# Expert routing of a two-layer decoder issued at other steps of the loop before it

## The reference

```python
x = _layernorm(x + attention(x))                       # phase 0: 16 heads
x = _layernorm(x + cross_attention_L0(x, context))     # phase 1: 16 heads, a norm of its own inside
x = _layernorm(x + experts_L0(x))                      # phase 2: top 2 of 8, GELU, hidden 512
x = _layernorm(x + gated_decay_attention(x))           # phase 3
x = _layernorm(x + cross_attention_L1(x, context))     # phase 4: 8 heads
x = _layernorm(x + experts_L1(x))                      # phase 5: top 1 of 8, ReLU, hidden 256

# experts_L0, its routing
router_logits = jnp.einsum('bth,eh->bte', x, router_w)
topk_values, topk_indices = jax.lax.top_k(router_logits, 2)
topk_weights = jax.nn.softmax(topk_values)
```

## Time and profile before

| what | value |
|---|---|
| median of 3 runs | 1522.08 us (1520.77 to 1522.19) |
| the profiled execution | 1532.61 us, of which the span of its instructions is 1530.8 us |
| PE, busy share of the span | 83% |
| ACT, busy share | 55% |
| DVE, busy share | 52% |
| POOL, busy share | 35% |
| mean granted TensorE clock | 0.927 of full |

### The profile page before, as it was taken

How to read it: one execution, slowest core, us unless ns; L and a number is a source line. 1 busy time by engine, 2 the same in 40 slices (tenths; PEclk the granted TensorE clock), 3 DMA queues, 4 the chain that set the end, 5 groups by cost and what they waited for, 6 DMA issues and landing times. The chain is left out here.

```text
span 1530.8 us, 22554 instructions
## 1 busy us (share of the span) xinstructions
PE 1276.4 (83%) x6934; PEld 735.2 (48%) x6934; DVE 801.0 (52%) x2448; ACT 839.1 (55%) x1902; POOL 530.0 (35%) x606
## 2 busy tenths in 40 slices
PE   5999999999999988877861994899999996786452
PEld 2334443444344335545431993576676764454251
DVE  3543454354334435366653235878675766567425
ACT  4777677767767753554430563567575653453121
POOL 2554455545545531212243351132223222112332
PEclk9999999999999999999885997999999997997686
DMA  8335343330000000000013671100000000000053
GB/s 211 57 62 83 63 71 60 57 80 1 1 1 1 1 1 0 1 1 0 3 58 131 195 208 48 42 1 1 1 1 1 1 1 28 0 1 8 23 153 100
DMA packets 77556, 67.29 MB, mean 44 GB/s; under 512 B 5024, under 2 KB 68640, under 8 KB 77184
## 3 DMA queue, kind: packets, MB, share of 16 engines
q1 hardware_dynamic: 73488, 57.69, 16.6%
q0 software_dynamic: 3520, 7.27, 1.3%
q10 hardware_dynamic: 432, 0.89, 0.2%
HBM read 37.42 MB, written 28.41 MB: 43 GB/s over the span
## 5 line engine op out<-in xcount | busy, mean ns | idle before, releaser
L1960 POOL TENSOR_TENSOR work<-work 128x512 f32<-128x512 f32 x256 | 266.1, 1039 | 271.6 <-DVE work L1438 271.6
L1013 ACT ACTIVATE work<-bank,work 128x512 f32<-128x512 f32 x256 | 176.5, 689 | 116.7 <-DVE work L1430 116.7
L1430 DVE TENSOR_REDUCE work<-bank 128x1 f32<-128x512 f32 x256 | 176.6, 690 | 77.5 <-PE bank L547 77.5
L555 PEld LDWEIGHTS bank<-cst,work 128*128 128x128 f32 x1024 | 110.4, 141 | 163.8 <-issue 103.5
L555 PE MATMUL bank<-cst,work 128*128 128x128 f32 x1024 | 159.7, 283 | 6.3 <-ACT work L1021 6.1
L1438 DVE RECIPROCAL work<-work 128x1 f32<-128x1 f32 x256 | 41.9, 164 | 223.4 <-ACT work L1013 223.1
L1021 ACT ACTIVATE work<-bank 128x512 f32<-128x512 f32 x256 | 152.6, 596 | 0.5 <-PE bank L555 0.5
L547 PE MATMUL bank<-work 64*128 64x512 f32 x512 | 144.5, 641 | 3.4 <-ACT work L1013 3.4
L2000 POOL TENSOR_TENSOR work<-work 128x1232 f32<-128x1232 f32 (+1 forms) x32 | 55.5, 1734 | 254.9 <-DVE work L1512 254.8
L565 PE MATMUL bank<-work 128*64 128x512 f32 x512 | 137.4, 617 | 0.7 <-ACT work L1021 0.7
L494 PE MATMUL bank<-OT,W 128*128 128x512 f32 x208 | 95.7, 604 | 1.2 <-DVE am L1618 0.7
(11 more groups left out here) (258 smaller groups left out, 2443.6 us busy)
## 6 DMA issues: line engine op xcount, KB each, us to landing
xs<-gat SPq DMA_DIRECT2D x18, 1040.0 KB, 13.1
W<-in_w SPq DMA_DIRECT2D x30, 322.0 KB
W<-in_w SPq DMA_DIRECT2D x23, 193.0 KB
work<-xs SPq DMA_DIRECT2D x62, 65.0 KB
gat<-yt SPq DMA_DIRECT2D x12, 256.0 KB, 3.4
work<-in_w SPq DMA_DIRECT2D x9, 322.0 KB
W<-in_v SPq DMA_DIRECT2D x1, 2048.0 KB, 12.3
x_ext<-in_x SPq DMA_DIRECT2D x4, 256.0 KB, 7.5
```

Of the source, the lines that this page charges most:

```text
L555: m = nc.tensor.transpose(out[:, k * P:(k + 1) * P], pA[u % 5][:, k * P:(k + 1) * P], ident)
L1013: A(pA[u % 5], bank[u % 3][:, :], ACT.Exp, bias=nmax[:, u % 8:u % 8 + 1], accum_out=rsum[0][:, u % 8:u % 8 + 1]).then_inc(sem("a_e"), 1)
L1430: V.tensor_reduce(nmax[:, u % 8:u % 8 + 1], bank[u % 3][:, :], AX, ALU.max, negate=True)\
L1960: G.tensor_tensor(pA[u % 5], pA[u % 5], rsum[1][:, u % 8:u % 8 + 1].to_broadcast([P, S]), ALU.mult)\
```

## The change

`cross` and `moe` issue the same instructions in another order; no operation is added or dropped. A piece in table form (steps u of the cross loop; "moe" is the head of the expert phase):

| piece | before | after |
|---|---|---|
| logits of batches 0, 1 (PE) | end of 11, 15 | end of 10, 14 |
| route1 of 0, 1 (DVE) | 12, 16, behind the tail pieces | 11, 15, ahead of them |
| exp of 0, 1 (ACT) | end of 12, 16 | end of 11, 15 |
| route2 of 0, 1 (DVE) | 13, 17 | 12, 16 |
| prefix of 0, 1 (PE) | end of 14, 18 | end of 13; 16 in phase 1, 17 in phase 4 |
| rank of 0, 1 (DVE) | 15; moe | 14; 16 in phase 1, 17 in phase 4 |
| scatter of batch 0 (POOL) | whole at 15 | half at 15, half at 16 |
| turn_x of batch 2 (PE, ACT) | 18 | 17, ahead of the output pairs of batch 3 |
| logits of batch 2 (PE) | moe | 17, between the second and the third output pair |
| prefix of 2 (PE) | behind the last output product | phase 2: ahead of it; phase 5: unchanged |

```diff
+        PREFIX_AT = {2: (13, 16), 5: (13, 17)}
+        RANK_AT = {2: (14, 16), 5: (14, 17)}
@@ cross_tail
-                        tail(w0 + b, s)
+                        if (b, s) != (NB - 2, 8):
+                            tail(w0 + b, s)
@@ PE, cross_out
-                for p in range(np_):
+                for p in pairs:
@@ PE, cross
-                    if t == 1 and b >= 1:
-                        cross_out(c, b - 1)
-                    if u in (11, 15):
+                    if u == PREFIX_AT[ph + 1][1]:
+                        moe_prefix(MOE[ph + 1], 1)
+                    if u == NB * NT + 1:
+
+                        tail(w0 + NB - 2, 8)
+                        cross_out(c, NB - 1, range(0, 2))
+                        moe_logits(MOE[ph + 1], NB - 2)
+                        cross_out(c, NB - 1, range(2, c["np"]))
+                    elif t == 1 and b >= 1:
+                        cross_out(c, b - 1, range(c["np"]))
+                    if u in (10, 14):
                         moe_logits(MOE[ph + 1], u // 4 - 2)
-                    if u in (14, 18):
-                        moe_prefix(MOE[ph + 1], u // 4 - 3)
+                    if u == PREFIX_AT[ph + 1][0]:
+                        moe_prefix(MOE[ph + 1], 0)
@@ PE, moe
-                moe_logits(m_, 2)
+                if ph == 2:
+                    moe_prefix(m_, 2)
                 tail(m_["w0"] - 1, 0)
-                moe_prefix(m_, 2)
+                if ph == 5:
+                    moe_prefix(m_, 2)
@@ ACT, cross
+                    if u == NB * NT + 1:
+                        tail(w0 + NB - 2, 8)
                     if t == 1 and b >= 1:
                         cross_o(c, b - 1)
-                    if u in (12, 16):
-                        moe_exp(MOE[ph + 1], u // 4 - 3)
+                    if u in (11, 15):
+                        moe_exp(MOE[ph + 1], u // 4 - 2)
@@ DVE, cross
+                    if u in (11, 15):
+                        moe_route1(MOE[ph + 1], u // 4 - 2)
                     cross_tail(tail, w0, u)
                     if u in (12, 16):
-                        moe_route1(MOE[ph + 1], u // 4 - 3)
-                    if u in (13, 17):
                         moe_route2(MOE[ph + 1], u // 4 - 3)
-                    if u == 15:
-                        moe_rank(MOE[ph + 1], 0)
+                    if u in RANK_AT[ph + 1]:
+                        moe_rank(MOE[ph + 1], RANK_AT[ph + 1].index(u))
@@ DVE, moe
-                moe_rank(m_, 1)
@@ POOL, cross
-                    if u == 15:
-                        moe_scatter(MOE[ph + 1], 0)
+                    if u in (15, 16):
+                        moe_scatter(MOE[ph + 1], 0, (0, 1) if u == 15 else (2, 3))
```

More of the change, by code:

```diff
@@ L657, in cross_turn, with cross_out @@
                     m.then_inc(sem(n + "_t"), 1)
-            def cross_out(c, b):
+            def cross_out(c, b, pairs):
                 n, np_ = c["n"], c["np"]
@@ L2002, in cross, with moe_scatter @@
                     cross_tail(tail, c["w0"], u)
-                    if u == 15:
-                        moe_scatter(MOE[ph + 1], 0)
-            def moe_scatter(m_, b):
+                    if u in (15, 16):
+                        moe_scatter(MOE[ph + 1], 0, (0, 1) if u == 15 else (2, 3))
+            def moe_scatter(m_, b, tiles=range(NT)):
                 pool.wait_ge(sem("M_idx"), m_["b0"] + b + 1)
@@ L2010, in moe_scatter @@
                     loaded(pool, "zero", DMA_COUNT["zero"])
-                for t in range(NT):
+                for t in tiles:
                     for k in range(m_["k"]):
```

## The result

The changed kernel took 1538.9 us (median of 4 runs, 1536.2 to 1541.3) against 1522.1 for the kernel before: ratio 1.0109, 95% interval 1.0093 to 1.0124. That is 16.8 us slower, with 14.2 to 18.9 as its interval; 21.7 was predicted, with a range that held the result. Its profiled execution took 1541.26 us, 1539.4 of it span.

The account below looks back on a forecast made before the run. PE was taken to be bound by waits for ACT, DVE and POOL in turn, not its own work. Terms 4.0 + 10.3 + 4.4 + 3.0 = 21.7 on 1522.1 gave 1544 us; range 1527 to 1551.

Parts of the forecast that it names:

- steps 1 to 4: Phase 1, up to DVE's unit 15: PE waits for shared banks' readers and ACT's copies; unit 15 comes 7.7 us later.
- steps 5, 6: Phase 1, after unit 15: POOL wins 7 us, but turn_x holds the pairs; batch 3's output product starts 5.0 us later.
- Step 7: End of phase 1: rank 2 is done before the last product's sum, -1.0 us.
- A page against a row: Whether scatter transfers hold DVE's normalisation: nothing by the trace rows, up to 4 us by the documented rule read widely.
- the narrow reading: POOL holds DVE's two-SBUF-input instructions only during its multiply, so the halved scatter costs DVE nothing.
- The clock: Phase 1: granted clock falls in four waits, each slowing the PE work behind it by 2.6 us, +10.3 in all.
- phase 1's sum: Phase 1 in total: +4.0 us without the clock and +10.3 us for the clock.
- Phase 4: The same waits with half the heads: batch 3's output product 4.4 us later, plus 3.0 us for the clock.
- the likeliest case: Whole kernel: new waits and slow clock behind them give 1544 us, bounds 1536 to 1551, chance 0.65.
- the waits come but the clock holds: Rival for both phases: clock falls at most once or twice; 8.4 us slower, up to 15, 1530 to 1536; chance 0.18.
- The faster rival: Bank readers finish in time and POOL's freeing pays: 5.5 to 10.4 us faster, 1512 to 1517; chance 0.11.
- steps 1 and 3: Phase 1 bank waits: second query product behind the logits copy, +4.3 us; batch 2's output product behind the rank, +7.5 us.

Follow-up runs that it names:

- e9: Changed kernel with shorter groups of unused PE products issued ahead of its waits, fewer in phase 4: 1542.1 us, 1.0134.
- e2: Changed kernel with logits and prefixes in PSUM bank 5 instead of a turn of banks 6 and 7: 1525.2 us, 1.0018.
- e4: Changed kernel with batch 0's rank ahead of DVE's subtraction of unit 14 instead of behind it and the norm: 1531.9 us, 1.0056.
- e10: Changed kernel with batch 0's logits, route1, exp and route2 back at their old steps: 1534.1 us, 1.0077.
- e1: The kernel before, run and profiled again without edit: 1522.6 us, 0.9996.
- e7: Changed kernel with logits 0, 1 and prefixes in bank 5 and the end of the cross phase in its old order: 1512.6 us, 0.9930.
- e12: Changed kernel with batch 0's scatter issued whole at step 15: 1543.9 us, 1.0149.
- e5: Changed kernel with unused PE products meant to fill its long waits; in the turns they stood behind the wait: 1538.7 us, 1.0116.
- e6: The kernel before with unused PE products meant to fill its long waits; in the turns they stood behind the wait: 1540.1 us, 1.0122.
- e8: Changed kernel with bank 5 for logits 0, 1 and prefixes, the old cross-phase end, and the scatter whole at step 15: 1522.1 us, 0.9993.
- e11: Changed kernel with turn_x and logits of batch 2 behind the last output pairs on PE and ACT: 1540.8 us, 1.0116.
- e3: The kernel before with logits and prefixes in bank 5: 1524.6 us, 1.0006.

## Why the prediction was right, and where its sizes were off

**The order of takes (steps 1 to 4): right.** Counted from DVE's unit 11 (701.4 in the working, 698.24 in the trace), the output product of batch 2 should start 48.0 later and unit 15 60.5 later. They came at 50.8 and 65.9. The products behind the first two waits ran 1.2 (8.27 for e9's 7.02) and 1.4 (7.22 for e9's 5.84) longer than at full clock, and the output product 2.6 (9.66 for 7.03); less these it is 48.2 and 60.7. e2, e4 and e10 show the cause: each wait goes with its own edit and takes its time with it.

**POOL freed, the pairs held by turn_x (steps 5, 6): right, one term missing.** POOL won its 7 us (e2: 7.2). From unit 15 to the end of `x_ext` the sum had 24.0; it took 26.3 (764.17 to 790.44). The 1.9 us for multiply 15 holding L1352 was right (2.10 for 0.16), but the same hold on L1575 (1.86 for 0.17) and on L1637 (1.02 for 0.22) was missing: 2.5 us. By the sum's own times multiply 14 starts at +4.8, just when DVE comes to route1, and the earlier trace rows showed what a multiply does to an instruction with two SBUF inputs.

**Step 7: right.** -1.0 predicted, -1.2 in B against e1.

**A page against a row: the trace decides for the narrow reading.** DVE's short instructions under the four transfers of 779 to 784 take 0.16 to 0.22 us, so the second half of the scatter costs DVE nothing. The held ones all overlap a multiply of POOL. That is what the Trainium skill, GPSIMD Engine Reference, "Key points", says of instructions with two SBUF inputs, and the Trainium skill, SBUF — State Buffer, "SBUF: two separate sides", says more narrowly that whichever of the two engines starts first has the shared ports for its whole instruction; the trace agrees (2.10 us for 0.16, ending with the multiply). One row does not fit so simply: L1353 of the earlier trace rows starts at 773.12, beside the last transfer and 0.56 us ahead of the multiply's recorded start at 773.68, and is held all the same. Which of the two had begun first is not shown, since spans on POOL are rough.

**The clock: the place right, the size too large.** Four falls of 2.6 were summed as +10.3. In the profile they cost 1.2, 1.4, 2.6 and, behind `turn_x`, 2.4 (12.3 us from the end of `x_ext`, 790.44, to the product, for 9.9 in the sum): 7.6. The term took the dearest fall of the earlier trace rows for each. Against that the earlier trace rows already held a fall at 678.15 that the changed kernel's execution did not have (5.67 for 8.27). So A closes, with the terms as the trace has them: 118.15 + 5.0 + 7.6 + 2.5 - 2.6 = 130.65, for 130.66 measured. That phase 1's sum came out so near (14.3; 14.1 with the clock and the holds as measured) is in part luck: the clock was put 2.7 us too high, and the missing holds 2.5 too low.

**Phase 4: too large.** 4.4 + 3.0 was predicted. The waits came as worked out: 1.99 for the query product (2.1), 3.30 for the output product (3.6), the pairs behind prefix 1 and rank 1. Counted from the start of C the output product came 7.6 us later than before (6.0 in the sum, which left the clock out) and the pairs 8.4 (5.5). Two things were less than the sum had them. The clock's term counted 1.75 for a slow output product behind its wait, and that one ran in 3.67 at a granted clock of 1.00 (1405 to 1415). And the clock came back earlier at the end than in the earlier trace rows: from the start of the last pairs to the last output product it is 6.76 us (9.50 before, 8.4 in the sum), so C grew by 5.6, and this product ran in 3.70, where it took 5.35 in the earlier trace rows and 5.36 in e1, so D shrank by 1.8. The sum had no term for a fall that goes away. Net 3.8 for 7.4.

Together the four stretches give 14.7 us for 21.7, and the medians 16.8. The result lies in the likeliest case's own bounds (1536 to 1551), near the end that had half of the clock's part. The rival "the waits come but the clock holds" falls for phase 1, where a slow product follows each of the waits; in phase 4 it is half right. The faster rival falls for the changed kernel, as steps 1 and 3 cost 13.7 us where it needed under 8. With them gone its time of 1512 to 1517 still did not come (e2: 1525.2), since `turn_x` holds the pairs. It was reached only with the end in its old order as well (e7: 1512.6).

**Open.** The 2.7 us (0.6 to 5.0) by which e2 is slower than the kernel before, though its stretches A to D are 2.2 us shorter than e1's in sum; and why e12 loses 5 us by the medians and 1.3 in A. Both gaps are as large as the profiled executions lie off their own medians: e2's 2.4 us below (it was the fastest of twelve) and e1's 2.2 above, e12's 1.9 below and the changed kernel's 2.4 above. What differs from one execution to the next is not shown. Open too is how much of the 16.8 us is the clock's: e9 won 5.6 us in phase 1 and lost 6.0 in phase 4, and e5 won 4.1 in A with no gain in its time. The fills of e5 and e6 were not repeated in the kernel before with their place mended.

## What to carry to other kernels

When a producer is moved earlier in a loop whose buffers go round in turn, list who takes the same buffer next and when its reader gets to read: two products that PE needed at once came to wait for a reader that stood behind 5 us of other work, and that cost more than the early start could bring. Freeing an engine pays only if the instruction next in line does not wait for something else: the same halved scatter was worth 9.5 us with the pairs first and 5.0 with `turn_x` first, of which the traces show 1.3 in its stretch. Take the price of a change as distances between two marks in the same stretch, from more than one execution, before any of it is put down to the clock.

## What the runs showed of the hardware

- A wait of the same length does not always cost clock: after 3.54 to 3.56 us of waiting, the same 24 matrix instructions of batch 1's pairs took 5.67 us in four executions (the changed kernel, e4, e8, e11), 7.03 to 7.22 in three (e1, e2, e7) and 8.27 to 8.49 in three (the kernel before, e3, e12). In phase 4 a wait of 3.24 was followed by 6.08 us for 16 of them, and one of 3.30 by an output product at full clock (3.67).
- DVE's instructions with two SBUF inputs are held until POOL's multiply is over, whatever their size: 128x4 elements took 1.86 and 2.10 us, 128x64 took 1.53 and 1.02. Each ended with the multiply, to within 0.1 us. One with a single SBUF tensor was held as well, the TENSOR_SCALAR L1360: 1.18 us at 733.90 for 0.17. MAX8 (0.37) ran beside the multiply unheld, and so did the sum L1634 of a PSUM and an SBUF operand (0.19 at 748.73).
- Beside POOL's indirect transfers DVE's small two-input instructions kept 0.16 to 0.24 us, but for those that ran in the last transfer of a scatter with a multiply right behind it. In eight such places one was held, from 0.54 to 0.61 us ahead of the multiply's recorded start until POOL's multiplies were over: 3.98 us in the earlier trace rows and in e1, 4.03 in e12, 3.96 in e8.
- In one execution of the fourteen profiled here B took 52.7 us, in all others 46.1 to 49.1. It was the one that the prediction was read from. In e1, the same program, B took 47.5; the difference is on DVE in the last tail, where from L1373 to L1363 it is 15.6 us there and 10.2 in e1.
